# Score products of the channel attention: sixteen ACT operations of 128 columns from PSUM in the place of one ACT copy and four VectorE products of 512

## The chip, the core and the metric

The kernel runs on one core of a Trainium2 chip. The metric is the device time of one execution in microseconds; the median of three runs is compared. Engines: PE is TensorE, ACT is ScalarE, DVE is VectorE, POOL is GpSimd, SP is the queue that issues most transfers. Each engine runs its own instruction stream in order; streams meet only at semaphores.

## What is computed

A decoder layer on x of 16 batches x 512 tokens x 512 channels, in float32: linear attention with a cumulative sum and a projection; cross attention over channels against `ctx`; one of eight feed-forward experts per batch, picked from the mean of the tokens; a layer norm after each. The change lies in the second part. Per batch, with four heads of 128 channels and two versions of per-channel weights and biases (global and local):

```python
scores = jnp.einsum('bhdn,bhen->bhde', q * wq + bq, k * wk + bk) * scale   # for (wqg, bqg, ...) and (wql, bql, ...)
attn = jax.nn.softmax(scores, axis=-1)
out = jnp.einsum('bhde,bhen->bhdn', attn, v * wv + bv)
```

The weights are numbers per channel, so the kernel computes one Gram product G[d, e] = sum over tokens of x[n, d] ctx[n, e] per head, the sums of ctx over tokens (a row C[e], the same on every partition) and those of x (a column), and puts both versions of the scores together from these: (wq[d] G[d, e] + bq[d] C[e]) wk[e], plus a term from the sums of x with bk. Here wq[d] and bq[d] are one number per partition and head, in the tile `cols`.

## The kernel before

Everything is one software pipeline over batches. Time is counted in half-steps: 32 to a batch (`HALVES`), and every engine walks the same double loop `for i ... for h ...`. In each half-step it first issues what `mix(i, h)` holds and then its share of the expert's feed-forward step. Plans such as `GRAM = plan(33)`, `SCORES = plan(34, 32)`, `CTX_ROW = plan(35, 33)` and `X_SUM = plan(36, 34)` give the half-step of each piece, counted from the start of the batch's own window, the later arguments for the first batches. So the score step of a batch c lies in the window of batch c + 1, beside that batch's `qkv` jobs (`JOB`, twelve products of twelve matmuls: for each block of channels k, v and q) and beside the feed-forward of an earlier batch.

The order around the change, for a middle batch:

- PE: a `qkv` job and `gram` (L1079, 32 matmuls into the bank M2, seen as `by_head`), a `down` (L1186, twelve matmuls); next half-step, job 2 (`q`, L1023 to L1025) and an `up` (L1170 to L1172, twelve matmuls); next, `ctx_sums` (L1086 and L1087, two matmuls into the same bank M2) and a `down`; next, job 3, `x_sums` (L1095, again into M2) and an `up`.
- ACT: in half-step 34 `feature` for job 2 (L485 `e_f`, L486 `r_f`, waits for `q_mm`), then `hidden` (L545 `hid`, waits for `up_mm`, and L552 `h_hi`); in 35 the copy `c_sb` of M2 (L568, waits for `c_mm`) and then `split_w` (L535 `we_hi`); in 36 `feature` for job 3, the column `s_x` (L574), `hidden`.
- DVE: in 34 `values`, then `scores_inner` (L784, two products of `by_head` with `cols` into `s_a`, waits for `g_mm`), `split_w` (L880 `we_lo`); in 35 `queries`, `numerator`, the low part of the hidden tile (L890 `h_lo`); in 36 `scores_ctx` (L789 two products of `c_sb` with `cols` into `a_v`, L792 two adds, L795 two products with a row of weights), later `scores_bias` and `scores_max`.

PE's `ctx_sums` overwrites M2, so it waits for both products of `scores_inner` (`sc_done`). `x_sums` overwrites it again, so it waits for the copy `c_sb` (`cb_done`). `up` of a step waits for `hid` of the one before (`h_done`), `down` for `h_hi` and `h_lo`. In the last batch no `qkv` job is left beside the score step.

Of the kernel before, what the change touches and what calls it, by code (L numbers as in the profile page):

```python
# [8 lines left out]
ALU = mybir.AluOpType  # L9
ACT = mybir.ActivationFunctionType  # L10
AX = mybir.AxisListType

P = 128
# [7 lines left out]
XH = 4  # L21
# [18 lines left out]
def upto(batch, per, n):  # L40
    due = min(batch * per + n, NB * per)
    return due if due > 0 else None
# [6 lines left out]
def plan(usual, *first):  # L49
    return np.array(list(first) + [usual] * (NB - len(first)))  # L50


def at(i, h, slot):
    return next((b for b in range(max(i - 3, 0), min(i + 2, NB)) if slot[b] == HALVES * (i - b) + h), None)
# [26 lines left out]
SCORES = plan(34, 32)  # L81
# [16 lines left out]
def build(nc, d, out):  # L98
    wq_dram = nc.dram_tensor("wq_scratch", [JOBS, P, 2 * CC * P], F32, kind="Internal").ap()

    with ExitStack() as ctx:
        def sb(name, shape, dt=F32):
            return ctx.enter_context(nc.sbuf_tensor(name, shape, dt))

        def sem(name):
            return ctx.enter_context(nc.semaphore(name))
# [21 lines left out]
        k_sum, kv_sum, q = sb("k_sum", [P, T]), sb("kv_sum", [P, T]), sb("q", [P, T])  # L128
        rows = sb("rows", [P, 8, C])
        WKG, BKG, WKL, BKL, WVG, BVG, WVL, BVL = range(8)  # L130
        c_sb = sb("c_sb", [P, XH, P])
        s_a, a_v = sb("s_a", [P, 2, XH, P]), sb("a_v", [P, 2, XH, P])
        aT = sb("aT", [P, XH, P])
        const_b = sb("const_b", [P, C])
# [7 lines left out]
        cols = sb("cols", [P, 6, XH])  # L142
        WQG, BQG, WQL, BQL, WP, BP = range(6)
        b_qkv, sb_qkv = sb("b_qkv", [P, 3 * CC]), sb("sb_qkv", [P, 3 * CC])
        scale = sb("scale", [P, 1])
# [21 lines left out]
        by_head = M2[:, :].rearrange("p (h e) -> p h e", h=XH)  # L167
# [26 lines left out]
        x1_done, x2_done, norm_done = sem("x1_done"), sem("x2_done"), sem("norm_done")  # L194
        high_done, low_done = sem("high_done"), sem("low_done")
        experts_done = sem("experts_done")
        g_mm, sx_mm, c_mm, cb_done = sem("g_mm"), sem("sx_mm"), sem("c_mm"), sem("cb_done")
        csum_done, diag_done, sx_done, sq_done = sem("csum_done"), sem("diag_done"), sem("sx_done"), sem("sq_done")
        sc_done, max_done, nmax_done, exp_done = sem("sc_done"), sem("max_done"), sem("nmax_done"), sem("exp_done")
        rec_done, rec2_done, av_done = sem("rec_done"), sem("rec2_done"), sem("av_done")  # L200
        asum_done, kall_done, kall2_done, diag2_done = (sem(n) for n in ("asum_done", "kall_done", "kall2_done", "diag2_done"))
        aT_mm, kb_mm, aT_done, kb_done, x1c_done = (sem(n) for n in ("aT_mm", "kb_mm", "aT_done", "kb_done", "x1c_done"))
# [15 lines left out]
        def bank(a, j):  # L218
            return (acc if a == 1 else AB)[j % 2]
# [250 lines left out]
        def _(act):  # L470
            def split_job(j):
                act.wait_ge(rq_in[j], 16)
                act.activation(held(j)[:, 0:C], staged(j), ACT.Copy).then_inc(wqhi_done, 1)

            def feature(a, cc, n):
                mm, done, col = ((k_mm, ek_done, CC + cc), (q_mm, eq_done, cc))[n]
                act.wait_ge(mm, CC * a + cc + 1)

                if n == 0:
                    if (due := upto(a, CC, cc)) is not None:  # L480
                        act.wait_ge(q_done, due)
                else:
                    act.wait_ge(k_done, CC * a + cc + 1)
                ps = bank(a, 3 * cc + 2 * n)
                act.activation(e_f[:, :], ps[:, :], ACT.Exp, bias=sb_qkv[:, col:col + 1], scale=scale[:, 0:1]).then_inc(done, 1)  # L485
                act.activation(r_f[:, :], ps[:, :], ACT.Relu, bias=sb_qkv[:, col:col + 1], scale=scale[:, 0:1]).then_inc(done, 1)  # L486
# [67 lines left out]
            def mix(i, h):  # L554
                if (b := at(i, h, FFN)) is not None:
                    split_x2(b, 3)
                for j, slot in enumerate(JOB):
                    if (a := at(i, h, slot)) is not None:
                        if a == 0 and 1 <= j <= JOBS - NQ:
                            split_job(j + NQ - 1)  # L560
                        if j % 3 != 1:
                            feature(a, j // 3, j % 3 // 2)
                if (c := at(i, h, CTX_ROW)) is not None:
                    act.wait_ge(c_mm, c + 1)

                    if (due := upto(c - 1, 12, 4)) is not None:
                        act.wait_ge(sc_done, due)
                    act.activation(c_sb[:, :, :], by_head, ACT.Copy).then_inc(cb_done, 1)  # L568
                if (c := at(i, h, X_SUM)) is not None:
                    act.wait_ge(sx_mm, c + 1)  # L570

# [84 lines left out]
        def _(dve):  # L656
# [45 lines left out]
            def numerator(a, cc):  # L702
                dve.wait_ge(q_done, CC * a + cc + 1)
                dve.wait_ge(kvc_done, CC * a + cc + 1)

                if a == 1:
                    dve.wait_ge(wplo_done, 1)
                elif a > 1:
                    dve.wait_ge(g_mm, a)
                dve.tensor_tensor(numer(a)[:, cc, :], q[:, :], kv_sum[:, :], ALU.mult).then_inc(num_done, 1)  # L710
# [61 lines left out]
            def row(n):  # L772
                return rows[:, n, :].rearrange("p (h e) -> p h e", h=XH)

            def per_channel(col):
                return col.unsqueeze(2).broadcast_to([P, XH, P])

            def scores_inner(c):
                dve.wait_ge(g_mm, c + 1)

                if (due := upto(c - 1, 4 * XH, 4 * XH)) is not None:
                    dve.wait_ge(av_done, due)
                for v, wqv in enumerate((WQG, WQL)):
                    dve.tensor_tensor(s_a[:, v, :, :], by_head, per_channel(cols[:, wqv, :]), ALU.mult).then_inc(sc_done, 1)  # L784

            def scores_ctx(c):
                dve.wait_ge(cb_done, c + 1)
                for v, bq in enumerate((BQG, BQL)):
                    dve.tensor_tensor(a_v[:, v, :, :], c_sb[:, :, :], per_channel(cols[:, bq, :]), ALU.mult).then_inc(sc_done, 1)  # L789
                dve.wait_ge(sc_done, 12 * c + 4)  # L790
                for v in range(2):
                    dve.tensor_tensor(s_a[:, v, :, :], s_a[:, v, :, :], a_v[:, v, :, :], ALU.add).then_inc(sc_done, 1)  # L792
                for v, wk in enumerate((WKG, WKL)):
                    dve.wait_ge(sc_done, 12 * c + 5 + v)
                    dve.tensor_tensor(s_a[:, v, :, :], s_a[:, v, :, :], row(wk), ALU.mult).then_inc(sc_done, 1)  # L795

            def token_sums(c):
# [5 lines left out]

            def scores_bias(c):
                dve.wait_ge(sq_done, 3 * c + 3)
                dve.wait_ge(sc_done, 12 * c + 6)
                for v, bk in enumerate((BKG, BKL)):
                    dve.tensor_tensor(a_v[:, v, :, :], row(bk), per_channel(s_q[:, v, :]), ALU.mult).then_inc(sc_done, 1)

            def scores_max(c):  # L810
                for v in range(2):
                    dve.wait_ge(sc_done, 12 * c + 9 + v)
                    dve.tensor_tensor(s_a[:, v, :, :], s_a[:, v, :, :], a_v[:, v, :, :], ALU.add).then_inc(sc_done, 1)
                for v in range(2):
                    dve.wait_ge(sc_done, 12 * c + 11 + v)
                    dve.reduce_max(neg_max[:, v, :], s_a[:, v, :, :], AX.X).then_inc(max_done, 1)
                for v in range(2):
                    dve.wait_ge(max_done, 2 * c + v + 1)
                    dve.tensor_scalar(neg_scaled[:, v, :], neg_max[:, v, :], -XSCALE, None, ALU.mult).then_inc(nmax_done, 1)
# [72 lines left out]
            def mix(i, h):  # L892
# [11 lines left out]
                for j, slot in enumerate(JOB):  # L904
                    if (a := at(i, h, slot + 1)) is not None:
# [5 lines left out]
                        if part == 2:  # L911
                            queries(a, cc)
                            numerator(a, cc)
                if (c := at(i, h, SCORES)) is not None:
                    scores_inner(c)
                if (c := at(i, h, CTX_ROW + 1)) is not None:
                    scores_ctx(c)
                if (c := at(i, h, X_SUM + 1)) is not None:
                    token_sums(c)
                    scores_bias(c)  # L920
# [78 lines left out]
        def _(pe):  # L999
# [82 lines left out]
            def ctx_sums(c):  # L1082
                pe.wait_ge(diag_done, c + 1)

                pe.wait_ge(sc_done, 12 * c + 2)
                pe.matmul(by_head, ones_r[:, :], diag[:, 0, :, :], start=True, stop=False)  # L1086
                pe.matmul(by_head, ones_r[:, :], diag[:, 1, :, :], start=False, stop=True).then_inc(c_mm, 1)  # L1087

            def x_sums(c):
                pe.wait_ge(xsum_done, (TT - 1) * c + TT - 1)  # L1090

                pe.wait_ge(cb_done, c + 1)
                for h in range(XH):
                    for k in range(0, P, SEG):
                        last = pe.matmul(col_ps[k:k + SEG, h, :], x_sum[:, h * P + k:h * P + k + SEG], ones[:, 0:SUM],  # L1095
                                         start=True, stop=True)
                last.then_inc(sx_mm, 1)
# [214 lines left out]
```

## Time and profile before

| | |
|---|---|
| median of 3 runs | 2385.33 us (2385.32 to 2385.66) |
| the profiled execution | 2383.82 us |
| its span in the trace | 2382.2 us |
| PE busy | 2332.2 us, 98% of the span |
| DVE busy | 1647.1 us, 69% |
| ACT busy | 1146.4 us, 48% |
| POOL busy | 504.1 us, 21% |
| TensorE clock granted over the span | 0.994 |

The span runs from the first to the last instruction that the trace holds. A matmul's row begins when it starts and overlaps the next one's: 512 columns last 0.39 us in a row and follow each other every 0.23 us. An "idle before" in brackets names what ended the idle time of that engine. The granted clock is 1.00 at 2.4 GHz and 0.50 at 1.2 GHz.

### The profile page before, as it was taken

What the parts mean: (1) busy time and instruction counts of PE and PEld (TensorE: products, weight loads), DVE (VectorE), ACT (ScalarE), POOL (GpSimd) and SP (SyncE); (2) the same over time, 40 slices, a digit from 0 to 9 for tenths busy, and PEclk for the clock granted to TensorE, in tenths of its full rate; (3) what the DMA queues carried; (4) which work ended last, traced back from release to release, by engine and by line L of the source; (5) the groups of instructions that cost most, each with busy time, mean ns of one, the idle gap of its engine ahead of it and who ended that gap; (6) DMA issues with size and microseconds to landing.
All of it is one profiled execution on the core that took longest, in us unless ns stands there. A gap on an engine that the chain in (4) does not pass through costs nothing.

```text
span 2382.2 us, 33918 instructions
## 1 busy us (share of the span) xinstructions
PE 2332.2 (98%) x11872; PEld 1923.2 (81%) x11872; DVE 1647.1 (69%) x2754; ACT 1146.4 (48%) x1905; POOL 504.1 (21%) x528
## 2 busy tenths in 40 slices
PE   7879999999999999999999999999999999999998
PEld 5668888888888888888888888888888888888787
DVE  8767586675867758587685866758677585775643
ACT  5344454445444545455445454454445454554553
POOL 3231212122121312113121221221213121131200
PEclk9989999999999999999999999999999999999999
DMA  8153456344354533546335463444635445453242
GB/s 302 62 159 128 155 149 208 106 177 133 137 197 124 191 119 142 177 124 203 116 142 169 135 210 101 181 130 137 203 123 187 124 142 177 124 159 98 100 119 82
DMA packets 96986, 354.74 MB, mean 149 GB/s; under 512 B 11826, under 2 KB 11954, under 8 KB 86706
## 3 DMA queue, kind: packets, MB, share of 16 engines
q1 hardware_dynamic: 79922, 319.02, 37.1%
q0 software_dynamic: 16896, 33.56, 8.8%
q8 instruction: 96, 1.57, 0.3%
q14 instruction: 72, 0.59, 0.1%
HBM read 329.47 MB, written 23.07 MB: 148 GB/s over the span
## 4 chain that ended last, share of the span: by engine, by line
PE 94%; DVE 3%; ACT 1%; issue 1%; POOL 1%; DMA 0%; SPq 0%; DVEq 0%; POOLq 0%; ACTq 0%
PE acc L1186 28%; PE h_ps L1170 10%; PE h_ps L1172 9%; PE h_ps L1171 9%; PE m L1023 7%; PE m L1025 7%; PE m L1024 7%; PE m L1063 2%; PE m L1065 2%; PE m L1064 2%; PE m L1079 2%; PE m L1139 2%; PE m L1153 1%; PE m L1049 1%; PE m L1036 1%
## 5 line engine op out<-in xcount | busy, mean ns | idle before, releaser
L545 ACT ACTIVATE hid<-h_ps,b 128x512 f32<-128x512 f32 x253 | 174.4, 689 | 620.4 <-PE h_ps L1172 619.6
L1170 PE MATMUL h_ps<-x2T_hi,we_hi 128*128 128x512 f32 x1012 | 402.1, 397 | 1.3 <-DVE x2T_lo L874 1.3
L1186 PE MATMUL acc<-we_hi,h_hi 128*128 128x512 f32 x1008 | 400.7, 398 | 1.6 <-DVE h_lo L890 1.6
L890 DVE TENSOR_TENSOR h_lo<-hid,h_hi 128x512 fp32r<-128x512 f32 x252 | 224.0, 889 | 252.3 <-ACT h_hi L552 252.3
L1172 PE MATMUL h_ps<-x2T_hi,we_lo 128*128 128x512 f32 x1012 | 394.6, 390 | 0.0
L1171 PE MATMUL h_ps<-x2T_lo,we_hi 128*128 128x512 f32 x1012 | 394.0, 389 | 0.0
L1186 PE MATMUL acc<-we_hi,h_lo 128*128 128x512 f32 x1008 | 393.1, 390 | 0.0
L1186 PE MATMUL acc<-we_lo,h_hi 128*128 128x512 f32 x1008 | 392.8, 390 | 0.0
L880 DVE TENSOR_TENSOR we_lo<-raw,we_hi 128x1024 fp32r<-128x1024 f32 x256 | 318.6, 1245 | 34.4 <-ACT we_hi L535 34.4
L485 ACT ACTIVATE e_f<-m,sb_qkv,scale 128x512 f32<-128x512 f32 x120 | 93.6, 780 | 481.7 <-PE m L1025 476.0
L1023 PE MATMUL m<-xT_hi,wq 128*128 128x512 f32 x684 | 268.5, 393 | 8.3 <-DVE wq L659 7.5
L535 ACT ACTIVATE we_hi<-raw 128x1024 fp32r<-128x1024 f32 x256 | 267.9, 1047 | 7.3 <-DMA raw<-in_w 7.3
L1025 PE MATMUL m<-xT_hi,wq 128*128 128x512 f32 x684 | 266.9, 390 | 0.0
L1024 PE MATMUL m<-xT_lo,wq 128*128 128x512 f32 x684 | 266.6, 390 | 0.0
L1170 PEld LDWEIGHTS h_ps<-x2T_hi,we_hi 128*128 128x128 f32 x1012 | 190.0, 188 | 42.6 <-issue 2.8
L1186 PEld LDWEIGHTS acc<-we_hi,h_hi 128*128 128x128 f32 x1008 | 189.4, 188 | 41.6 <-issue 3.0
L1172 PEld LDWEIGHTS h_ps<-x2T_hi,we_lo 128*128 128x128 f32 x1012 | 189.9, 188 | 40.5
L1186 PEld LDWEIGHTS acc<-we_hi,h_lo 128*128 128x128 f32 x1008 | 189.2, 188 | 40.3
L1171 PEld LDWEIGHTS h_ps<-x2T_lo,we_hi 128*128 128x128 f32 x1012 | 190.2, 188 | 37.0
L1186 PEld LDWEIGHTS acc<-we_lo,h_hi 128*128 128x128 f32 x1008 | 189.5, 188 | 37.0
L552 ACT ACTIVATE h_hi<-hid 128x512 fp32r<-128x512 f32 x252 | 159.5, 633 | 8.0
L1023 PEld LDWEIGHTS m<-xT_hi,wq 128*128 128x128 f32 x684 | 128.7, 188 | 36.0 <-issue 9.9
(230 smaller groups left out, 3628.6 us busy)
## 6 DMA issues: line engine op xcount, KB each, us to landing
raw<-in_w SPq DMA_DIRECT2D x256, 512.0 KB, 4.1
wq<-wq_scratch SPq DMA_DIRECT2D x168, 512.0 KB, 3.3
x<-in_x_tok SPq DMA_DIRECT2D x16, 1024.0 KB, 5.5
x<-in_b_proj POOLq DMA_DIRECT2D x16, 1024.0 KB, 14.9
ctx_T<-in_ctxT SPq DMA_DIRECT2D x16, 1024.0 KB, 8.8
ctx_tok<-in_ctx_tok SPq DMA_DIRECT2D x16, 1024.0 KB, 4.8
x<-in_b POOLq DMA_DIRECT2D x16, 1024.0 KB, 11.6
out_dram<-x SPq DMA_DIRECT2D x15, 1024.0 KB, 4.8
```

Of the source, the lines that this page charges most:

```text
L535: act.activation(we_hi[:, g % NW, :], raw[:, g % NR, :], ACT.Copy).then_inc(whi_done, 1)
L545: act.activation(hid[:, f % 2, :], up_bank(b, f)[:, :], ACT.Relu, bias=b1[:, b % 2, f:f + 1]).then_inc(h_done, 1)
L552: act.activation(h_part(h_hi, xT_hi, b, f), hid[:, f % 2, :], ACT.Copy).then_inc(hhi_done, 1)
L880: dve.tensor_tensor(we_lo[:, g % NW, :], raw[:, g % NR, :], we_hi[:, g % NW, :].bitcast(F32), ALU.subtract).then_inc(wlo_done, 1)
L890: dve.tensor_tensor(h_part(h_lo, xT_lo, b, f), hid[:, f % 2, :], h_part(h_hi, xT_hi, b, f).bitcast(F32), ALU.subtract).then_inc(hlo_done, 1)
L1023: pe.matmul(bank(a, j)[:, :], w[:, 0, t, :], x_hi[:, t, :], start=(t == 0), stop=False)
L1024: pe.matmul(bank(a, j)[:, :], w[:, 0, t, :], x_lo[:, t, :], start=False, stop=False)
L1025: last = pe.matmul(bank(a, j)[:, :], w[:, 1, t, :], x_hi[:, t, :], start=False, stop=(t == CC - 1))
L1170: pe.matmul(ps, we_hi[:, g % NW, js], x2T_hi[:, j, :], start=(j == 0), stop=False)
L1171: pe.matmul(ps, we_hi[:, g % NW, js], x2T_lo[:, j, :], start=False, stop=False)
L1172: last = pe.matmul(ps, we_lo[:, g % NW, js], x2T_hi[:, j, :], start=False, stop=(j == CC - 1))
L1186: last = pe.matmul(acc[t][:, :], hx[:, f % 2, ts], wx[:, g % NW, C:], start=(f == 0 and n == 0), stop=(f == FC - 1 and n == 2))
```

## The change

ACT now makes both sets of products that have one number per channel. In half-step 34, behind `feature` and ahead of `hidden`, it reads M2 in eight operations of 128 columns (two versions x four heads), each an Identity with a column of `cols` as its scale, into `s_a`. In half-step 35 eight more read the row of ctx sums from M2 into `a_v`, in the place of the copy `c_sb`, ahead of `split_w`. The tile `c_sb`, `scores_inner` and the two products of `scores_ctx` on DVE are gone; its adds wait for the four heads of their version on both semaphores, `inner_done` and `row_done`. PE's `ctx_sums` waits for all eight of the first set, `x_sums` for all eight of the second. `sc_done` counts eight a batch instead of twelve.

```diff
--- before.py
+++ after.py
@@ -128,7 +128,6 @@
         k_sum, kv_sum, q = sb("k_sum", [P, T]), sb("kv_sum", [P, T]), sb("q", [P, T])
         rows = sb("rows", [P, 8, C])
         WKG, BKG, WKL, BKL, WVG, BVG, WVL, BVL = range(8)
-        c_sb = sb("c_sb", [P, XH, P])
         s_a, a_v = sb("s_a", [P, 2, XH, P]), sb("a_v", [P, 2, XH, P])
         aT = sb("aT", [P, XH, P])
         const_b = sb("const_b", [P, C])
@@ -194,8 +193,9 @@
         x1_done, x2_done, norm_done = sem("x1_done"), sem("x2_done"), sem("norm_done")
         high_done, low_done = sem("high_done"), sem("low_done")
         experts_done = sem("experts_done")
-        g_mm, sx_mm, c_mm, cb_done = sem("g_mm"), sem("sx_mm"), sem("c_mm"), sem("cb_done")
+        g_mm, sx_mm, c_mm = sem("g_mm"), sem("sx_mm"), sem("c_mm")
         csum_done, diag_done, sx_done, sq_done = sem("csum_done"), sem("diag_done"), sem("sx_done"), sem("sq_done")
+        inner_done, row_done = sem("inner_done"), sem("row_done")
         sc_done, max_done, nmax_done, exp_done = sem("sc_done"), sem("max_done"), sem("nmax_done"), sem("exp_done")
         rec_done, rec2_done, av_done = sem("rec_done"), sem("rec2_done"), sem("av_done")
         asum_done, kall_done, kall2_done, diag2_done = (sem(n) for n in ("asum_done", "kall_done", "kall2_done", "diag2_done"))
@@ -560,12 +560,25 @@
                             split_job(j + NQ - 1)
                         if j % 3 != 1:
                             feature(a, j // 3, j % 3 // 2)
+                if (c := at(i, h, SCORES)) is not None:
+                    act.wait_ge(g_mm, c + 1)
+
+                    if (due := upto(c - 1, 4 * XH, 4 * XH)) is not None:
+                        act.wait_ge(av_done, due)
+                    if (due := upto(c - 1, 1, 1)) is not None:
+                        act.wait_ge(asum_done, due)
+                        act.wait_ge(aT_mm, due)
+                    for v, wqv in enumerate((WQG, WQL)):
+                        for hd in range(XH):
+                            act.activation(s_a[:, v, hd, :], by_head[:, hd, :], ACT.Identity,
+                                           scale=cols[:, wqv, hd:hd + 1]).then_inc(inner_done, 1)
                 if (c := at(i, h, CTX_ROW)) is not None:
                     act.wait_ge(c_mm, c + 1)
 
-                    if (due := upto(c - 1, 12, 4)) is not None:
-                        act.wait_ge(sc_done, due)
-                    act.activation(c_sb[:, :, :], by_head, ACT.Copy).then_inc(cb_done, 1)
+                    for v, bq in enumerate((BQG, BQL)):
+                        for hd in range(XH):
+                            act.activation(a_v[:, v, hd, :], by_head[:, hd, :], ACT.Identity,
+                                           scale=cols[:, bq, hd:hd + 1]).then_inc(row_done, 1)
                 if (c := at(i, h, X_SUM)) is not None:
                     act.wait_ge(sx_mm, c + 1)
 
@@ -775,23 +788,13 @@
             def per_channel(col):
                 return col.unsqueeze(2).broadcast_to([P, XH, P])
 
-            def scores_inner(c):
-                dve.wait_ge(g_mm, c + 1)
-
-                if (due := upto(c - 1, 4 * XH, 4 * XH)) is not None:
-                    dve.wait_ge(av_done, due)
-                for v, wqv in enumerate((WQG, WQL)):
-                    dve.tensor_tensor(s_a[:, v, :, :], by_head, per_channel(cols[:, wqv, :]), ALU.mult).then_inc(sc_done, 1)
-
             def scores_ctx(c):
-                dve.wait_ge(cb_done, c + 1)
-                for v, bq in enumerate((BQG, BQL)):
-                    dve.tensor_tensor(a_v[:, v, :, :], c_sb[:, :, :], per_channel(cols[:, bq, :]), ALU.mult).then_inc(sc_done, 1)
-                dve.wait_ge(sc_done, 12 * c + 4)
                 for v in range(2):
+                    dve.wait_ge(inner_done, 2 * XH * c + XH * v + XH)
+                    dve.wait_ge(row_done, 2 * XH * c + XH * v + XH)
                     dve.tensor_tensor(s_a[:, v, :, :], s_a[:, v, :, :], a_v[:, v, :, :], ALU.add).then_inc(sc_done, 1)
                 for v, wk in enumerate((WKG, WKL)):
-                    dve.wait_ge(sc_done, 12 * c + 5 + v)
+                    dve.wait_ge(sc_done, 8 * c + 1 + v)
                     dve.tensor_tensor(s_a[:, v, :, :], s_a[:, v, :, :], row(wk), ALU.mult).then_inc(sc_done, 1)
 
             def token_sums(c):
@@ -803,16 +806,16 @@
 
             def scores_bias(c):
                 dve.wait_ge(sq_done, 3 * c + 3)
-                dve.wait_ge(sc_done, 12 * c + 6)
+                dve.wait_ge(sc_done, 8 * c + 2)
                 for v, bk in enumerate((BKG, BKL)):
                     dve.tensor_tensor(a_v[:, v, :, :], row(bk), per_channel(s_q[:, v, :]), ALU.mult).then_inc(sc_done, 1)
 
             def scores_max(c):
                 for v in range(2):
-                    dve.wait_ge(sc_done, 12 * c + 9 + v)
+                    dve.wait_ge(sc_done, 8 * c + 5 + v)
                     dve.tensor_tensor(s_a[:, v, :, :], s_a[:, v, :, :], a_v[:, v, :, :], ALU.add).then_inc(sc_done, 1)
                 for v in range(2):
-                    dve.wait_ge(sc_done, 12 * c + 11 + v)
+                    dve.wait_ge(sc_done, 8 * c + 7 + v)
                     dve.reduce_max(neg_max[:, v, :], s_a[:, v, :, :], AX.X).then_inc(max_done, 1)
                 for v in range(2):
                     dve.wait_ge(max_done, 2 * c + v + 1)
@@ -911,8 +914,6 @@
                         if part == 2:
                             queries(a, cc)
                             numerator(a, cc)
-                if (c := at(i, h, SCORES)) is not None:
-                    scores_inner(c)
                 if (c := at(i, h, CTX_ROW + 1)) is not None:
                     scores_ctx(c)
                 if (c := at(i, h, X_SUM + 1)) is not None:
@@ -1082,14 +1083,14 @@
             def ctx_sums(c):
                 pe.wait_ge(diag_done, c + 1)
 
-                pe.wait_ge(sc_done, 12 * c + 2)
+                pe.wait_ge(inner_done, 2 * XH * c + 2 * XH)
                 pe.matmul(by_head, ones_r[:, :], diag[:, 0, :, :], start=True, stop=False)
                 pe.matmul(by_head, ones_r[:, :], diag[:, 1, :, :], start=False, stop=True).then_inc(c_mm, 1)
 
             def x_sums(c):
                 pe.wait_ge(xsum_done, (TT - 1) * c + TT - 1)
 
-                pe.wait_ge(cb_done, c + 1)
+                pe.wait_ge(row_done, 2 * XH * c + 2 * XH)
                 for h in range(XH):
                     for k in range(0, P, SEG):
                         last = pe.matmul(col_ps[k:k + SEG, h, :], x_sum[:, h * P + k:h * P + k + SEG], ones[:, 0:SUM],
```

## Rows read from the trace of the kernel before

**Rows 1.** the page, chain of work that ended last, shares by engine

```profile
PE 94%; DVE 3%; ACT 1%; issue 1%; POOL 1%; DMA 0%; SPq 0%; DVEq 0%; POOLq 0%; ACTq 0%
```

**Rows 2.** busy times by stretch: from:to, length, each engine's busy us, PEclk, DMA, GB/s

```profile
241.00:2182.00 1941.00, 1940.23 (x9947) 1604.40 (x9945) 1363.84 (x2281) 950.28 (x1583) 407.10 (x407) 1.00 0.47 152
```

**Rows 3.** timeline of ACT, batch 6: start us, us, engine, line, operation, idle before

```profile
893.22 0.78 ACT L485 ACTIVATE e_f<-m,sb_qkv,scale 128x512 f32<-128x512 f32 x1 [9.44 <-PE m L1025]
...
893.90 0.77 ACT L486 ACTIVATE r_f<-m,sb_qkv,scale 128x512 f32<-128x512 f32 x1
...
895.94 0.69 ACT L545 ACTIVATE hid<-h_ps,b 128x512 f32<-128x512 f32 x1 [1.27 <-PE h_ps L1172]
...
896.66 0.64 ACT L552 ACTIVATE h_hi<-hid 128x512 fp32r<-128x512 f32 x1
...
897.20 0.58 ACT L568 ACTIVATE c_sb<-m 128x512 f32<-128x512 f32 x1
```

**Rows 4.** the same timeline of PE and DVE, batch 6

```profile
894.14 1.26 DVE L784 TENSOR_TENSOR s_a<-m,cols 128x512 f32<-128x512 f32 x2
...
895.74 0.39 PE L1086 MATMUL m<-diag,ones_r 128*128 128x512 f32 x1
...
901.73 0.46 PE L1095 MATMUL m<-ones,x_sum 128*32 128x32 f32 x32
```

**Rows 5.** groups by line and shape, ACT: count, busy us, mean ns, idle before

```profile
L535 ACT ACTIVATE we_hi<-raw 128x1024 fp32r<-128x1024 f32 x256 | 267.9, 1047 | 7.3 <-DMA raw<-in_w 7.3
...
L552 ACT ACTIVATE h_hi<-hid 128x512 fp32r<-128x512 f32 x252 | 159.5, 633 | 8.0
...
L516 ACT ACTIVATE s_a<-s_a,neg_scaled 128x128 f32<-128x128 f32 x128 | 49.4, 387 | 4.0 <-DVE neg_scaled L819 4.0
```

**Rows 6.** timeline, batches 2 and 14: `r_f` on ACT, first matmul of `ctx_sums`

```profile
314.69 0.77 ACT L486 ACTIVATE r_f<-m,sb_qkv,scale 128x512 f32<-128x512 f32 x1
...
316.53 0.39 PE L1086 MATMUL m<-diag,ones_r 128*128 128x512 f32 x1
...
2052.33 0.77 ACT L486 ACTIVATE r_f<-m,sb_qkv,scale 128x512 f32<-128x512 f32 x1
...
2054.17 0.39 PE L1086 MATMUL m<-diag,ones_r 128*128 128x512 f32 x1
```

**Rows 7.** timeline, batch 1: `r_f`, `c_sb` on ACT, `x_sums` on PE

```profile
179.65 0.77 ACT L486 ACTIVATE r_f<-m,sb_qkv,scale 128x512 f32<-128x512 f32 x1
...
180.32 0.60 ACT L568 ACTIVATE c_sb<-m 128x512 f32<-128x512 f32 x1
...
184.76 0.46 PE L1095 MATMUL m<-ones,x_sum 128*32 128x32 f32 x32
```

**Rows 8.** timeline, batch 0, on DVE, PE and ACT

```profile
81.31 1.29 DVE L784 TENSOR_TENSOR s_a<-m,cols 128x512 f32<-128x512 f32 x2 [2.69 <-PE m L1079]
...
82.74 0.47 PE L1086 MATMUL m<-diag,ones_r 128*128 128x512 f32 x1 [1.47 <-DVE s_a L784]
...
83.47 0.60 ACT L568 ACTIVATE c_sb<-m 128x512 f32<-128x512 f32 x1 [5.58 <-PE m L1087]
...
86.84 1.29 DVE L792 TENSOR_TENSOR s_a<-s_a,a_v 128x512 f32<-128x512 f32 x2
...
100.49 0.79 PE L1023 MATMUL acc<-x2T_hi,we_lo 128*128 128x512 f32 x1 [5.52 <-DVE kv_sum L682]
```

**Rows 9.** timeline, batch 15: `c_sb` on ACT, `x_sums` and a `down` on PE

```profile
2193.83 0.58 ACT L568 ACTIVATE c_sb<-m 128x512 f32<-128x512 f32 x1
...
2195.64 0.46 PE L1095 MATMUL m<-ones,x_sum 128*32 128x32 f32 x32
...
2217.35 0.47 PE L1186 MATMUL acc<-we_hi,h_hi 128*128 128x512 f32 x1 [1.55 <-DVE h_lo L890]
```

**Rows 10.** busy times by stretch, after two waits of PE; last but two is PEclk

```profile
100.00:107.00 7.00, 6.51 (x16) 5.12 (x17) 6.86 (x21) 0.00 (x0) 1.82 (x3) 0.52 0.01 3
...
2215.00:2223.00 8.00, 6.45 (x31) 5.17 (x30) 6.53 (x10) 4.45 (x7) 5.66 (x6) 1.00 0.19 67
```

## The prediction

> **What bounds the kernel now.** I read the page first: TensorE (PE) holds 94% of the chain that ended last [rows 1]. ScalarE (ACT) and VectorE (DVE) matter only where PE waits for them. Second, where PE waits at all: from 241 to 2182 us, the stretch with the score steps of batches 2 to 14, PE is busy 1940.23 of 1941 us [rows 2]. No slack there can swallow a new wait, and no wait there can be removed: whatever holds PE in this stretch is added to the end. The waits that exist lie in the start (batches 0 and 1) and in the tail. Third, the timeline around one score step (batch 6) on ACT, DVE and PE [rows 3, 4], to see how far ahead of PE the two results are that the change moves.
>
> The score step has two handovers to PE, both over the one PSUM bank M2. Before `ctx_sums` may overwrite the Gram products, somebody must have read them; before `x_sums` may overwrite the row of ctx sums, somebody must have read that. Now DVE does the first in two operations of 512 columns: it starts at 894.14 and ends at 895.40 [rows 4], 0.34 us before `ctx_sums` starts at 895.74. ACT does the second in one copy `c_sb`, 897.20 to 897.78 [rows 3]; `x_sums` starts at 901.73 [rows 4], so there are 3.95 us to spare.
>
> **The price of a new ACT operation.** None in the trace is 128 columns, from PSUM, with a scale per partition. The bounds come from neighbours. Columns: 1024 of them take 1047 ns and 512 take 633 ns for the same kind of copy [rows 5], so 384 columns fewer are (1047 - 633) x 384 / 512 = 311 ns. Two operands per partition, from PSUM, 512 columns: `r_f` 770 ns [rows 3], so 128 columns make 0.46 us. With one such operand: `hid` 690 ns [rows 3], so 0.38 us; the Exp of 128 columns with one, from SBUF, is 387 ns [rows 5] and agrees. The next operation starts before the last one ends: `e_f` to `r_f` is 0.68 for a duration of 0.78 [rows 3], and after `r_f` the next start is again 0.67 later (179.65 to 180.32 in batch 1) [rows 7]. So eight in a row take 7 x 0.36 + 0.46 = 2.98 us with two operands, 7 x 0.28 + 0.38 = 2.34 us with one, and 8 x 0.46 = 3.68 us if they did not overlap. The diff gives each a scale column and no bias. Whether the missing bias is read as a column too, the trace can't say; the Exp and Relu rows here all name a tile as their bias (`sb_qkv`, `b`, `neg_scaled`) [rows 3, 5], so none shows one without. I take two operands, the case nearest to `r_f`, and keep the other two for the range.
> The Trainium skill (ScalarE: Activation LUTs, section "What ACT_TABLE_LOAD costs") prices such an operation from its fixed part, columns and pointer operands; that would be an estimated 479 ns each and 386 ns from start to start, so 3.18 us for eight and some 2.6 us more over the 13 stalls below. The same page ("Rules for kernel authors") would keep products on VectorE. The trace does not bear it out per element (a PSUM copy of 512 on ACT is 0.58 us [rows 3], a product on DVE 1.26 for two [rows 4]); what costs here is the split into eight pieces.
>
> **Edit 1, the inner products go to ACT: the cost.** In ACT's program order they stand in the same half-step as, and behind, `feature` of job 2, which waits for the last matmul of `q`. ACT is idle for 9.44 us ahead of `e_f` [rows 3], but the eight can't use that: they are issued after `r_f`. So in batch 6 they start at 893.90 + 0.67 = 894.57 and end at 897.55. In batch 0 PE took 0.14 us from the end of DVE's result (81.31 + 1.29 = 82.60) to its start at 82.74, and that matmul lasted 0.47 instead of 0.39 [rows 4, 8]. So `ctx_sums` starts at 897.69 instead of 895.74 and 0.08 is lost at its restart: a stall of 1.95 + 0.08 = 2.03 us. The distance from `r_f` to `ctx_sums` is 1.84 us in batch 2 (314.69 to 316.53) and in batch 14 (2052.33 to 2054.17) as in batch 6 [rows 3, 4, 6], and so in all 13 batches from 2 to 14: 13 x 2.03 = 26.4 us.
>
> **What queues behind them on ACT.** `hid` of the step starts at 897.5 instead of 895.94 and `h_hi` ends near 898.8. Their readers are the next `up` (it needs `h_done`), which stands behind `x_sums`, and a `down` later still; nothing is late.
>
> **Edit 2, the row products go to ACT: hidden.** `c_sb` (0.58 us) goes, eight products come; they start behind `h_hi` as `c_sb` did, near 898.76, and end near 901.75. `x_sums` would be due at 897.69 + 0.08 + (901.73 - 895.74) = 903.8 [rows 4]: 2 us to spare. The cover is one `down` and one `qkv` of twelve matmuls, some 2.7 us each (the 5.99 us hold them and the two matmuls of `ctx_sums`); with either gone, as in batches 0 and 15, there is a wait. The split of weights `we_hi` behind them starts near 901.65, some 4 us later than now, for the `up` after the next, which is four blocks of 2.7 us behind `x_sums`.
>
> **Edit 3, DVE loses four products a batch.** The two inner ones take 1.26 us [rows 4] and the two from `c_sb` about the same, some 2.5 us x 16 = 40 us of DVE work. The add of version 1 must wait for the last row product (901.75), so DVE's chain `s_a` ends about as late as now relative to PE or earlier. Worth nothing in the stretch where PE does not wait for DVE [rows 2].
>
> **The batches that differ.** Batch 1: the job with a feature stands a half-step earlier and the inner products have two blocks on PE to run beside; the row products start at 180.32 and end at 183.3, ahead of `x_sums` at 184.76 [rows 7]: nothing. Batch 0: inner products start with the Gram end at 81.31, end at 84.29, `ctx_sums` is 1.7 us late; `c_sb` started 0.73 after it, so row products run from 85.16 to 88.14. What PE loses there (some 2.2 us) falls into its wait of 5.52 us for DVE at 100.49 [rows 8]; only DVE's delay is left. Its add of version 1 starts at 88.2 instead of 86.84 + 0.61 = 87.45: +0.8 us. Batch 15: no job, so inner products are free, but there is only the down block between `ctx_sums` and `x_sums`: row products from 2193.83 to 2196.81, `x_sums` at 2196.95 + 0.08 instead of 2195.64, a loss of 1.4 us. A wait of 1.55 us for DVE's `h_lo` follows at 2217.35 [rows 9] and gives about 1.0 back, as DVE itself is only some 0.4 us late: +0.4 us.
>
> **Sum.** 26.4 + 0.8 + 0.4 = 27.6 us on a profiled span of 2382.2, so 2409.8. That execution took 2383.82 in all and the median is 2385.33, 3.1 above the span: 2385.33 + 27.6 = 2413.
>
> **Rivals.** *One operand.* If the missing bias costs nothing, the eight end at 896.91 and the stall is 1.31 + 0.08 = 1.39 us: 18 us for 13 and about 0.3 for batches 0 and 15, 2404 us. For it: `hid` at 690 [rows 3]. Chance 0.13. *No overlap*, or a price above the neighbours: eight in 3.68 us, a stall of 2.7 us, 35.5 and 2 for the ends, 2423 us. Against it: the 0.68 steps [rows 3]. Chance 0.09.
> *The clock.* After PE's idle of 5.52 us at 95 to 100.5 its granted clock is 0.52 from 100 to 107, near its lower level of 1.2 GHz; across the wait of 1.55 at 2217 it stays at 1.00, 2.4 GHz [rows 8 to 10]. The new stalls are 2.03 us, nearer to the second. If each brought the slower clock for those 7 us, 3.4 would be lost 13 times: 44 us more, 2457 us. Chance 0.03.
> The Trainium skill (TensorE: Matmul & The Clock Gate, "Why this matters for your kernels") also warns of idle gaps between bursts of matmuls; the trace agrees for the idle of 5.52 us [rows 8, 10], and no row here shows one of 2 us.
> *Not slower.* The mechanism is ACT's idle 9.44 us before `e_f`: if the eight ran in it or took no more than 895.74 - 0.14 - 894.57 = 1.03 us (0.13 each), `ctx_sums` would not move. The same holds if `ctx_sums` didn't wait for all eight. Then batches 0 and 15 are all that is left, with DVE relieved by up to 1.3 us ahead of the wait of 5.52: 2384 to 2386 us. Against it: the program order and the wait on `inner_done` in the diff, and that even a shortest case (584 - 311 = 273 ns, 0.18 apart, so 1.5 us for eight) still stalls PE by 0.6 us, 8 us in all. Chance 0.04, of which 0.01 for a real gain elsewhere.
>
> **How the numbers follow.** Forecast 2413 us, chance 0.70; the rivals 0.13, 0.09, 0.03, 0.04; 0.01 for slower in a way I don't see. Range 2402 to 2425: from just under the one-operand case to just over the no-overlap case, leaving out the clock case and the unmoved one. A difference under 0.2% (4.8 us) can't be told from none: slower 0.95, same 0.04, faster 0.01.
>
> **What would show it.** In the profile of the changed kernel: PE waits for ACT `s_a` on the line of the first matmul of `ctx_sums`, 13 times near 2 us, outside batches 1 and 15; eight Identity of 128 columns between `r_f` and `hid`, 0.36 us apart, 0.46 each; no wait before `x_sums` in batches 2 to 14, one in batch 15; PE's clock unchanged; DVE some 40 us less busy. A spacing of 0.28 or 0.46 gives the second or third time. No such waits, or the eight products ahead of `e_f`, would make the forecast wrong; so would a wait before `x_sums` in the middle batches, since I hold 2 us of cover there.

## The result

The changed kernel takes 2402.07 us (median of 4 runs, 2400.56 to 2403.62) against 2385.32: 16.8 us slower, a ratio of 1.0073 with a 95% interval of 1.006 to 1.0085. The forecast was 2413 us, 27.6 slower; the direction and the place are as forecast, the size is 0.6 of it. The profiled execution took 2403.62, the longest of the four, with a span of 2402.0, 19.8 us over the span of before; so sums over the trace come out some 3 us above the difference of the medians.

The page of the changed kernel: busy time by engine, then the chain that ended last.

```profile
PE 2338.5 (97%) x11872; PEld 1925.0 (80%) x11872; DVE 1613.6 (67%) x2690; ACT 1203.5 (50%) x2145; POOL 505.7 (21%) x528
...
PE 93%; ACT 3%; DVE 2%; issue 1%; POOL 1%; DMA 0%; ACTq 0%; DVEq 0%; POOLq 0%
```

DVE has lost 33.5 us of busy time, ACT has gained 57.1, and ACT's share of the chain has gone from 1% to 3%, with PE and DVE one point lower each (before: [rows 1]). Who waited for whom on PE (us in all, times, longest), the first rows and the one on `x_sums`:

```profile
PE m L1087 <- ACT s_a L573: 15.1, 14, 2.4
PE m L1050 <- ACT rden_all L623: 10.5, 1, 10.5
...
PE acc L1024 <- DVE kv_sum L695: 4.0, 1, 4.0
PE acc L1024 <- ACT r_f L486: 2.1, 1, 2.1
...
PE m L1096 <- ACT a_v L580: 0.4, 1, 0.4
```

The first row is the change: L1087 is the first matmul of `ctx_sums`, L573 the inner products; before, PE waited on this line only in batch 0, 1.47 us for DVE [rows 8]. The row on `r_f` lies in batch 0 and is taken up further down. The timeline of ACT in batch 6, with the groups of the two sets of products (mean ns last but one):

```profile
901.25 0.78 ACT L485 ACTIVATE e_f<-m,sb_qkv,scale 128x512 f32<-128x512 f32 x1 [9.45 <-PE m L1026]
901.93 0.77 ACT L486 ACTIVATE r_f<-m,sb_qkv,scale 128x512 f32<-128x512 f32 x1
902.60 2.17 ACT L573 ACTIVATE s_a<-m,cols 128x128 f32<-128x128 f32 x8
904.60 0.76 ACT L545 ACTIVATE hid<-h_ps,b 128x512 f32<-128x512 f32 x1
905.38 0.63 ACT L552 ACTIVATE h_hi<-hid 128x512 fp32r<-128x512 f32 x1
905.92 2.16 ACT L580 ACTIVATE a_v<-m,cols 128x128 f32<-128x128 f32 x8
...
L573 ACT ACTIVATE s_a<-m,cols 128x128 f32<-128x128 f32 x128 | 34.8, 394 | 5.9 <-PE m L1080 5.9
L580 ACT ACTIVATE a_v<-m,cols 128x128 f32<-128x128 f32 x128 | 34.6, 382 | 1.2 <-PE m L1088 1.2
```

The order is the one foretold: ACT idles 9.45 us ahead of `e_f`, then the eight follow `r_f` (compare [rows 3]). They take 2.17 us, though, not 2.98. On PE, `ctx_sums` of batches 2, 6 and 14 and `x_sums` of batch 6:

```profile
320.78 0.47 PE L1087 MATMUL m<-diag,ones_r 128*128 128x512 f32 x1 [0.98 <-ACT s_a L573]
904.92 0.47 PE L1087 MATMUL m<-diag,ones_r 128*128 128x512 f32 x1 [0.98 <-ACT s_a L573]
911.02 0.46 PE L1096 MATMUL m<-ones,x_sum 128*32 128x32 f32 x32
2073.09 0.47 PE L1087 MATMUL m<-diag,ones_r 128*128 128x512 f32 x1 [0.98 <-ACT s_a L573]
```

A wait of 0.98 in each of 13 batches. A row's idle counts from the end of the row before, which lasts 0.16 beyond the usual start of the next (0.39 against 0.23), and the restart costs 0.08, so the loss is 1.22. The period says the same: from batch 2 to 14 the twelve periods take 1752.31 us, 146.03 each, against (2054.17 - 316.53) / 12 = 144.80 before [rows 6]: 1.22 us more. There is no wait at `x_sums`: the row products end at 908.08, 2.94 us ahead of it.

The 19.8 us of the profiled execution are then: 15.9 in batches 2 to 14 (13 x 1.22); 3.1 ahead of them, some 1.2 of which arose before the change comes into play (PE's granted clock was low for longer near 50 us, in that execution); 0.8 in the tail. Of the 16.8 us between the medians, 15.9 leave 0.9 for both ends together.

### The profile page after: what moved, and what is told of

Read it like the earlier page. It is cut to its first block, busy times and chain, and to the rows that moved or that the text cites. A ratio compares the mean times of both kernels' runs of the same rounds, so it can differ in the third digit from the quotient of the medians.

```text
span 2402.0 us, 34126 instructions
## 1 busy us (share of the span) xinstructions
PE 2338.5 (97%) x11872; PEld 1925.0 (80%) x11872; DVE 1613.6 (67%) x2690; ACT 1203.5 (50%) x2145; POOL 505.7 (21%) x528
## 4 chain that ended last, share of the span: by engine, by line
PE 93%; ACT 3%; DVE 2%; issue 1%; POOL 1%; DMA 0%; ACTq 0%; DVEq 0%; POOLq 0%
PE acc L1187 28%; PE h_ps L1171 9%; PE h_ps L1173 9%; PE h_ps L1172 9%; PE m L1024 7%; PE m L1026 7%; PE m L1025 7%; PE m L1064 2%; PE m L1066 2%; PE m L1065 2%; PE m L1080 2%; PE m L1140 2%; ACT s_a L573 1%; PE m L1154 1%; PE m L1037 1%
```

## Does the place in ACT's queue cause the loss?

My theory after the result: PE waits for the last inner product, which stands behind `q` in ACT's program order. The rival: sixteen more operations are a load on ACT, which makes `hid`, `h_hi` and the weights late wherever they stand.

**The inner products ahead of `feature`.** One block moved:

```diff
+                if (c := at(i, h, SCORES)) is not None:
+                    act.wait_ge(g_mm, c + 1)
...
                 for j, slot in enumerate(JOB):
...
-                if (c := at(i, h, SCORES)) is not None:
-                    act.wait_ge(g_mm, c + 1)
...
```

> The changed kernel with one edit: ACT issues the eight inner products ahead of `feature` of the same half-step, so in the idle time before `e_f`. Theory (program order: the whole loss of the middle batches is PE's wait for the last inner product, which stands behind `q` in ACT's queue): the eight start when the Gram product ends, some 5 us before they are needed; no PE wait at the first matmul of `ctx_sums` in batches 2 to 14; 13 x 1.23 = 16 us are back, 2386 us (2385 to 2389), with batch 0 as in the changed kernel. Rival (load: sixteen operations more on ACT delay `hid`, `h_hi` and the weights, wherever they stand): at least half the loss stays, 2394 us or more.

Measured: 2385.35 us against 2384.28 for the kernel before, ratio 1.0004 (0.9995 to 1.0014). ACT in batch 6:

```profile
890.77 2.18 ACT L567 ACTIVATE s_a<-m,cols 128x128 f32<-128x128 f32 x8 [3.99 <-PE m L1080]
896.23 0.78 ACT L485 ACTIVATE e_f<-m,sb_qkv,scale 128x512 f32<-128x512 f32 x1 [3.28 <-PE m L1026]
896.91 0.77 ACT L486 ACTIVATE r_f<-m,sb_qkv,scale 128x512 f32<-128x512 f32 x1
```

and on PE `ctx_sums` of batch 6, which starts 5.8 us after the last inner product has ended and waits for nothing, and the waits at `ctx_sums` and `x_sums` that are left, in batches 0 and 15:

```profile
898.75 0.39 PE L1087 MATMUL m<-diag,ones_r 128*128 128x512 f32 x1
...
84.93 0.55 PE L1087 MATMUL m<-diag,ones_r 128*128 128x512 f32 x1 [2.36 <-ACT s_a L567]
...
2198.83 0.46 PE L1096 MATMUL m<-ones,x_sum 128*32 128x32 f32 x32 [0.43 <-ACT a_v L580]
```

The same sixteen operations on the same engine, with eight of them at another place in the queue: the loss is gone, as far as the runs can tell. The load rival, which kept half of it, has fallen.

**Each half alone.** Only the row products on ACT; and only the inner ones:

```diff
-                    for v, wqv in enumerate((WQG, WQL)):
-                        for hd in range(XH):
-                            act.activation(s_a[:, v, hd, :], by_head[:, hd, :], ACT.Identity,
-                                           scale=cols[:, wqv, hd:hd + 1]).then_inc(inner_done, 1)
...
+            def scores_inner(c):
+                dve.wait_ge(g_mm, c + 1)
...
+                    dve.tensor_tensor(s_a[:, v, :, :], by_head, per_channel(cols[:, wqv, :]), ALU.mult).then_inc(inner_done, 1)
```

> Half of the change: only the eight row products are on ACT (the copy and its two DVE products are gone), the inner products stay on DVE. Theory (program order): they are covered by a `down` and a `qkv` job, no wait before `x_sums` in batches 2 to 14, only some 0.4 us in batch 15 and part of a microsecond in batch 0: 2386 us (2384.5 to 2388). Rival (load): half the operations, half the loss, 2393 us. Second rival (DVE's relief is worth something): below 2384.5.

```diff
-                    for v, bq in enumerate((BQG, BQL)):
-                        for hd in range(XH):
-                            act.activation(a_v[:, v, hd, :], by_head[:, hd, :], ACT.Identity,
-                                           scale=cols[:, bq, hd:hd + 1]).then_inc(row_done, 1)
...
+                    act.activation(c_sb[:, :, :], by_head, ACT.Copy).then_inc(row_done, 1)
...
+                    dve.tensor_tensor(a_v[:, v, :, :], c_sb[:, :, :], per_channel(cols[:, bq, :]), ALU.mult).then_inc(rp_done, 1)
```

> The other half: only the eight inner products are on ACT, at the place of the change; the row goes through the copy and two DVE products as before. Theory (program order): all 13 waits of about 1 us at `ctx_sums` are there, 2401 us (2399 to 2403). Rival (load): half the loss, 2393 us.

Measured: row products alone 2383.57 against 2384.28, ratio 0.9998 (0.9988 to 1.0007); inner products alone 2400.61, ratio 1.0067 (1.005 to 1.0084), with all the waits at `ctx_sums` in place (us in all, times, longest):

```profile
PE m L1090 <- ACT s_a L574: 15.1, 14, 2.4
```

Eight operations in the one place cost all, eight in the other cost nothing that can be told. The first result, row products alone, lies 0.9 us under my range, where I had put the second rival, that DVE's relief is worth something. The range was set against 2385.33, and the kernel before took 2384.28 beside these runs, so most of the 0.9 may be that. Still, the trace has a cause that I had priced at nothing: PE's wait for DVE near 100 us is 4.20 instead of 5.52 [rows 8], since DVE has two products less just there.

```profile
83.88 0.47 PE L1088 MATMUL m<-diag,ones_r 128*128 128x512 f32 x1 [1.47 <-DVE s_a L788]
100.31 0.79 PE L1025 MATMUL acc<-x2T_hi,we_lo 128*128 128x512 f32 x1 [4.20 <-DVE kv_sum L686]
```

So DVE's relief is worth about 1.3 us in batch 0 of that trace, and 0.6 go again at `x_sums` of batch 15; the comparison can't tell the rest from zero.

## What does one operation cost?

The inner products get a bias tile of zeros, so they name two operands per partition. The row products lose their scale and name none; this kernel leaves out the factor bq.

```diff
-                            act.activation(s_a[:, v, hd, :], by_head[:, hd, :], ACT.Identity,
+                            act.activation(s_a[:, v, hd, :], by_head[:, hd, :], ACT.Identity, bias=zcol[:, 0:1],
                                            scale=cols[:, wqv, hd:hd + 1]).then_inc(inner_done, 1)
...
-                            act.activation(a_v[:, v, hd, :], by_head[:, hd, :], ACT.Identity,
-                                           scale=cols[:, bq, hd:hd + 1]).then_inc(row_done, 1)
+                            act.activation(a_v[:, v, hd, :], by_head[:, hd, :], ACT.Identity).then_inc(row_done, 1)
```

> What one operation costs. The inner products get an explicit bias tile of zeros (same result); the row products lose their scale (the products with bq are left out, so the scores are without the factor bq). Reading A (a missing bias costs nothing, one operand counts): with the bias tile the eight stand 0.34 us apart instead of 0.25, the PE wait grows from 0.98 by about 0.6 us, some 2410 us. Reading B (a missing bias is read as an operand as well): nothing changes in the inner products, wait 0.98, 2402 us. By either, the row products without scale show what one operand costs: 0.25 us apart as now if operands are hidden at 128 columns, 0.16 to 0.18 if each costs some 0.09.

Measured: 2412.03 us (one run). Batch 6 on ACT, the groups, and PE:

```profile
905.36 2.89 ACT L574 ACTIVATE s_a<-m,zcol,cols 128x128 f32<-128x128 f32 x8
...
909.40 1.44 ACT L581 ACTIVATE a_v<-m 128x128 f32<-128x128 f32 x8
...
L574 ACT ACTIVATE s_a<-m,zcol,cols 128x128 f32<-128x128 f32 x128 | 46.3, 475 | 5.9 <-PE m L1081 5.9
L581 ACT ACTIVATE a_v<-m 128x128 f32<-128x128 f32 x128 | 23.0, 300 | 0.9 <-PE m L1089 0.9
...
908.40 0.47 PE L1088 MATMUL m<-diag,ones_r 128*128 128x512 f32 x1 [1.70 <-ACT s_a L574]
```

Reading A holds. From PSUM, 128 columns, an operation lasts 300 ns with no operand per partition, 382 to 394 with one, 475 with two; eight in a row take 1.44, 2.17 and 2.89 us, so they start 0.16, 0.25 and 0.35 us apart. Each operand costs some 0.09 us, and a bias that is not given costs none. The Trainium skill (ScalarE: Activation LUTs, "What ACT_TABLE_LOAD costs") states about 93 ns for a pointer operand, and the trace agrees. The overlap of one operation with the next is 0.13 to 0.14 us here, more than the 93 ns that the Trainium skill gives in the same section, and than the 0.10 that I read off the pair of 512 columns.

With two operands the wait is 1.70, so 0.72 more where I expected 0.6, and the loss 1.93 a batch, near the 2.03 of my sum: the mechanism carries the number once the operand is put in.

## Dose: more operations in either place

```diff
+                    for hd in range(XH):
+                        act.activation(spare[:, hd, :], by_head[:, hd, :], ACT.Identity,
+                                       scale=cols[:, WQG, hd:hd + 1]).then_inc(inner_done, 1)
                     for v, wqv in enumerate((WQG, WQL)):
```

> The changed kernel with four more operations of the same kind ahead of the eight inner products (into a spare tile; result as before), so twelve between `r_f` and `ctx_sums`. Theory (PE waits for the last one, at 0.255 us each, and the clock stays): the wait of batches 2 to 14 grows from 0.98 by 1.02 to 2.0 us, 13 x 1.02 = 13.3 us more, and up to 2 in batch 0: 2416 us (2414 to 2418). Rival (clock: a wait of 2 us in a middle batch lowers TensorE's clock for a while, as the wait of 2.36 us in batch 0 of the changed kernel did for 3.4 us): 1.7 us more in each of 13, 2438 us.

Measured: 2422.54 us (ratio 1.0158, 1.0143 to 1.0174), 6.5 us over the theory and above its range, and 15 under the rival. The waits of batches 2 to 14 are as forecast, and still the periods are not all alike. `ctx_sums` of three batches, and stretches behind it (PEclk last but two):

```profile
911.17 0.47 PE L1093 MATMUL m<-diag,ones_r 128*128 128x512 f32 x1 [2.01 <-ACT s_a L579]
1058.25 0.47 PE L1093 MATMUL m<-diag,ones_r 128*128 128x512 f32 x1 [2.01 <-ACT s_a L579]
1206.96 0.47 PE L1093 MATMUL m<-diag,ones_r 128*128 128x512 f32 x1 [2.01 <-ACT s_a L579]
...
910.00:914.00 4.00, 2.83 (x12) 2.36 (x13) 1.82 (x3) 3.97 (x14) 0.00 (x0) 1.00 0.44 135
1058.00:1062.00 4.00, 3.75 (x12) 2.98 (x13) 1.87 (x3) 3.97 (x12) 0.00 (x0) 0.70 0.14 58
1942.00:1946.00 4.00, 3.65 (x11) 2.98 (x12) 1.77 (x3) 3.97 (x12) 0.00 (x0) 0.70 0.24 97
```

From 911.17 to 1058.25 is 147.08 us, from 1058.25 to 1206.96 it is 148.71. After two of the thirteen waits of 2.01 us the granted clock fell towards its lower level, 1.2 GHz, and 1.6 us were lost each time; after eleven it stayed at 2.4 GHz. The sum of this trace: 13 x 2.26 = 29.4, 3.3 for the clock, 4.3 ahead of batch 2, together 37.0 of the 37.7 us between the spans. So both theories hold in part. In the changed kernel (waits of 0.98) and with the bias tile (1.70) all twelve periods are equal within 0.1 us.

```diff
+                    for n in range(4 * XH):
+                        act.activation(spare[:, n, :], by_head[:, n % XH, :], ACT.Identity,
+                                       scale=cols[:, BQG, n % XH:n % XH + 1]).then_inc(row_done, 1)
                     for v, bq in enumerate((BQG, BQL)):
```

> The changed kernel with sixteen more operations of the same kind ahead of the eight row products (into a spare tile; result as before). Theory (the row products are hidden only by one `down` and one `qkv` block: in batch 6 the last ends at 908.08 and `x_sums` starts at 911.02, 2.94 us later): sixteen more take 4.06 us, so 1.27 + 0.08 us of wait before `x_sums` in each of 13 batches, 17.5 us, near 2 in batch 1, some 3 to 4 in batch 15 and 2 in batch 0: 2426 us (2422 to 2430). Rival (ACT work at this place is free): 2402 us.

Measured: 2432.48 us (ratio 1.0196, 1.018 to 1.0212). PE in batch 6, then `x_sums` of batches 1 and 15:

```profile
915.47 0.47 PE L1093 MATMUL m<-diag,ones_r 128*128 128x512 f32 x1 [0.97 <-ACT s_a L574]
922.90 0.46 PE L1102 MATMUL m<-ones,x_sum 128*32 128x32 f32 x32 [1.28 <-ACT a_v L586]
...
191.66 0.46 PE L1102 MATMUL m<-ones,x_sum 128*32 128x32 f32 x32 [1.92 <-ACT a_v L586]
...
2241.62 0.65 PE L1102 MATMUL m<-ones,x_sum 128*32 128x32 f32 x32 [4.55 <-ACT a_v L586]
```

The cover is what it was held to be: 1.28 us of wait against 1.27 worked out from the slack of 2.94. The time is 6 us over the theory and above its range, and most of that lies in the ends. The sixteen operations were priced against the changed kernel: ahead of batch 2 they cost 5.5 us more than it (248.97 against 243.52 at the same `attend` of batch 1), where I had put 4, and the tail costs 7.0 us more, where I had put 3 to 4. There PE's wait of 4.55 at `x_sums` makes 4.1, and the granted clock of 0.50 over the 4 us behind it goes with the rest.

## What is left, and a version without it

With the order mended, batch 0 remains: there ACT needs 2.18 us where DVE needed 1.29 [rows 8], PE waits 2.36 us, and its granted clock falls behind that wait. Stretches of the changed kernel (PEclk last but two):

```profile
84.00:86.00 2.00, 1.16 (x3) 0.96 (x4) 0.19 (x1) 0.84 (x4) 0.00 (x0) 0.77 0.00 0
86.00:88.00 2.00, 2.00 (x6) 1.56 (x5) 0.69 (x1) 2.00 (x8) 0.00 (x0) 0.50 0.01 4
88.00:90.00 2.00, 2.00 (x30) 1.36 (x33) 1.86 (x3) 0.12 (x2) 0.00 (x0) 0.88 0.04 8
```

So the last version keeps the moved block and gives the inner products of batch 0 back to DVE:

```diff
-                if (c := at(i, h, SCORES)) is not None:
+                if (c := at(i, h, SCORES)) is not None and c > 0:
                     act.wait_ge(g_mm, c + 1)
...
+                if at(i, h, SCORES) == 0:
+                    scores_inner(0)
```

> The kernel with the inner products ahead of `feature`, and those of batch 0 alone left on DVE. Theory (what is left of the change's loss once the order is mended is batch 0: ACT needs 2.2 us there for what DVE does in 1.3, PE waits 2.36 instead of 1.47 and its clock falls for 3.4 us after it): PE waits 1.47 at `ctx_sums` of batch 0, its clock stays, DVE's chain there is as short as with only the row products moved: 2383.5 us, 0.5 to 1.5 under the kernel before or not to be told from it. Rival (order and load do cost something in the middle): 2385 us or more.

Measured: 2383.98 us against 2384.98, ratio 0.9995 (0.9986 to 1.0004). PE in batch 0:

```profile
82.84 0.47 PE L1100 MATMUL m<-diag,ones_r 128*128 128x512 f32 x1 [1.47 <-DVE s_a L794]
99.27 0.50 PE L1034 MATMUL acc<-x2T_hi,we_lo 128*128 128x512 f32 x1 [4.21 <-DVE kv_sum L695]
...
84.00:88.00 4.00, 4.00 (x49) 3.05 (x48) 4.00 (x6) 3.26 (x10) 0.00 (x0) 1.00 0.03 6
```

The wait is 1.47 again and the clock stays up from 84 to 88, as expected, but no version beats the kernel before by what the runs can tell. The theory had one thing wrong: the slow clock behind `ctx_sums` of batch 0 was no part of the loss. In the changed kernel PE stood 2.10 us behind the kernel before at `ctx_sums` (84.84 against 82.74) and 2.15 behind at its next wait, for `kv_sum` (102.64 against 100.49): the slow stretch went into that wait. What was lost later lies behind a wait for `r_f` in the same batch. The kernel before, the changed one and this last version:

```profile
110.11 0.50 PE L1023 MATMUL acc<-x2T_hi,h_hi 128*128 128x512 f32 x1 [0.56 <-ACT r_f L486]
110.00:114.00 4.00, 3.47 (x14) 2.55 (x14) 3.78 (x4) 1.38 (x4) 0.00 (x0) 1.00 0.38 131
...
112.26 0.70 PE L1024 MATMUL acc<-x2T_hi,h_hi 128*128 128x512 f32 x1 [2.10 <-ACT r_f L486]
112.00:116.00 4.00, 3.74 (x9) 2.94 (x10) 3.62 (x4) 0.69 (x2) 0.00 (x0) 0.57 0.12 49
...
108.90 0.50 PE L1034 MATMUL acc<-x2T_hi,h_hi 128*128 128x512 f32 x1 [1.84 <-ACT r_f L486]
110.00:114.00 4.00, 3.97 (x11) 2.77 (x9) 2.76 (x3) 0.56 (x1) 0.00 (x0) 0.57 0.00 0
```

From this matmul to PE's next wait (for `const_b`) it is 5.1 us in the three traces in which the wait for `r_f` was 0.56, 0.67 or 1.11 us, and 6.6 to 6.7 in the six in which it was 1.82 or more. In the last version that takes back the 1.3 us that DVE's relief gave. Which of the two happens is not settled by the edit: the way from the wait for `kv_sum` to this one is 9.6 us in all nine traces, and PE waits little there where its granted clock stayed low for longer in between. With the inner products alone it waited 3.99 us for `kv_sum`, much as in the changed kernel (3.97), but then the clock was 0.50 up to 108 us, and the wait for `r_f` was only 0.67; in the changed kernel the clock was back at 1.00 by 106. Why the slow stretch ended earlier in one than in the other stays open.

That nothing is won is also in line with [rows 2]: with PE busy 1940.23 of 1941 us there is nothing in the middle to win by relieving DVE.

## Why the prediction came out as it did

- *What bounds the kernel.* Right. Every wait put on PE in the middle appears in the time: 13 x 1.22 = 15.9 of the 16.8 us.
- *Edit 1, the place.* Right, and shown by moving it: behind `r_f`, in the queue behind `q`, with 9.45 us of idle ACT that it can't use.
- *Edit 1, the size.* This term was mis-sized. I took two operands per partition and 2.98 us for eight; it is one operand and 2.17 us. The one-operand rival (2.34 us, a stall of 1.39, 2404 us), to which I gave 0.13 against 0.70 for the forecast, was the case that came, with a stall of 1.22 and 2402 us. The range was drawn to take this case in and began at 2402; that 2402.07 lies in it is by a hair, and luck. I chose by the neighbour `r_f`, whose bias and scale are both columns; the diff itself names one column only, and of the rows I had `hid`, with one operand, was the like one. That the eight overlap by 0.14 us and not 0.10 gives the rest.
- *Edit 2, hidden.* Right: no wait at `x_sums` in batches 2 to 14, 2.94 us to spare (2 were forecast with the longer operations), and sixteen operations more overran it by the 1.28 us that this slack gives.
- *Edit 3, DVE's relief worth nothing.* Right for the middle; wrong by about 1.3 us for batch 0 of the versions that leave its inner products on DVE, where PE does wait for DVE. DVE's busy time fell by 33.5 us, where I had worked out 40.
- *Batch 0 and 15.* I gave 0.8 and 0.4, together 1.2, and the medians leave 0.9. The path in batch 0 is as forecast up to the wait for `kv_sum`: from before `ctx_sums` to there the profiled run loses 0.9 us. The slower clock behind the wait for `r_f` then costs 1.6, of which 0.7 comes back near 140 us, where the clock stayed low for less long than before, so that it is 1.9 in all. In batch 15 PE loses 0.5 at `x_sums`, and the 1.0 that I took to be given back at the wait for `h_lo` is not: that wait is 1.55 us as before. Another 0.3 goes at a later wait for DVE (`x`), 0.8 in all.
- *The clock rival.* It had its grain of truth: it did not happen at the waits of 0.98, but it did at 2.36 and at 2.10 in batch 0, and at two of thirteen waits of 2.01 with twelve operations. Whether my stalls of 2.03 us would have lost clock is not shown: as the trace counts, such a stall is a wait of 1.79 us (0.24 less), and the nearest at this place, 1.70, lost none in 13.

## What to carry to other kernels

On a kernel whose bounding engine never idles, a step moved to an idle engine costs nothing only if it ends before its reader is due: ask what stands ahead of it in the queue, and how much time is left behind it, not how busy the engine is. Count the tiles per partition that each small ACT operation names, since at 128 columns each is about a third of the step from one to the next. And write out, for each handover, how long the result is ready before its reader; 0.34 us for the one and 3.95 us for the other decided here which half of the edit costs.

## What the runs showed of the hardware

The unexpected part is the clock near waits of two microseconds. Waits of PE of 0.98 and 1.70 us in the middle were followed by no fall of the granted clock in 13 cases each; waits of 2.01 by a fall in two of 13; one of 1.92 in batch 1 (24 row operations) by a granted clock of 0.75 over the next 4 us; those of 1.82 to 3.18 for `r_f` in batch 0 by a fall in six of six, those of 0.56 to 1.11 at the same place by none in three; those of 2.36 at `ctx_sums` in batch 0 by a fall in each of three traces, in the changed kernel by 3.4 us or so at half speed (the rows at 84 to 90 us above), though the kernel with 24 row operations kept 1.00 from 84 to 90 after a wait of 2.35 at the same matmul. So the length of the wait alone does not tell these cases apart, nor does the work ahead of it, which is the same for 2.35 and 2.36. What does tell them apart is left open.
